# Inverted row sums are spread over their head's 64 rows through a DRAM scratch row instead of by TensorE transpositions

## The reference

```python
q  = norm(x) @ Wqa @ Wqb               # 16 heads, 128 plain + 64 rotary columns
ckv = norm(x) @ Wkva                    # 64 latent columns (keys and values) + 64 rotary ones
scores = (q_h @ k_h.T) * scale          # causal, 1024 x 1024 for each head
attn = softmax(scores)                  # exp(scores - max) / row sum
out  = attn @ v                         # v comes out of the 64 latent columns
x = x + out @ Wout
x = x + experts(norm(x))                # router, 64 experts in 8 groups, top 8
```

## Time and profile before

| | |
|---|---|
| median of 3 runs | 1745.24 us (1744.07 to 1745.45) |
| span of the profiled execution | 1743.9 us |
| attention, bodies 1 to 31 | about 36 us each, 31 times |
| PE busy | 1690.3 us, 97% |
| DVE / ACT / POOL busy | 1237.6 / 982.1 / 572.6 us |

### The profile page before, as it was taken

How to read it: one execution, slowest core, us unless ns; L and a number is a source line. 1 busy time by engine, 2 the same in 40 slices (tenths; PEclk the granted TensorE clock), 3 DMA queues, 4 the chain that set the end, 5 groups by cost and what they waited for, 6 DMA issues and landing times. The chain is left out here.

```text
span 1743.9 us, 32128 instructions
## 1 busy us (share of the span) xinstructions
PE 1690.3 (97%) x11280; PEld 1384.5 (79%) x11280; DVE 1237.6 (71%) x2858; ACT 982.1 (56%) x2319; POOL 572.6 (33%) x498
## 2 busy tenths in 40 slices
PE   5799999999999999999999999999999999999998
PEld 4677777778777777777777777777699999999998
DVE  6878788778788788787887878877654454555543
ACT  6566666666666666666666666666533333433332
POOL 4553344434443344433344334434401110110100
PEclk9899999999999999999999999999999999999999
DMA  8300000012000003000001100001200000000000
GB/s 285 123 7 7 7 14 7 8 30 76 13 8 7 7 7 103 8 7 7 9 12 49 56 7 14 7 7 42 81 1 25 25 1 25 25 13 13 13 13 13
DMA packets 35868, 51.45 MB, mean 30 GB/s; under 512 B 2368, under 2 KB 26944, under 8 KB 35712
## 3 DMA queue, kind: packets, MB, share of 16 engines
q1 hardware_dynamic: 35712, 49.39, 8.7%
HBM read 35.23 MB, written 14.16 MB: 28 GB/s over the span
## 5 line engine op out<-in xcount | busy, mean ns | idle before, releaser
L1296 ACT ACTIVATE probs<-aps,nmax 128x384 f32<-128x384 f32 (+7 forms) x512 | 378.8, 744 | 215.9 <-DVE nmax L1353 210.1
L1353 DVE CUSTOM_DVE_ANT_0 aps<-aps,mask_row 128x384 f32<-128x384 f32 (+7 forms) x512 | 388.6, 770 | 132.0 <-PE aps L43 125.7
L1222 PE MATMUL aps<-ident,probs 128*128 128x128 f32 x2304 | 329.1, 272 | 0.8 <-ACT probs L1296 0.6
L43 PE MATMUL aps<-kTh,qh 128*128 128x512 f32 (+3 forms) x768 | 293.6, 382 | 8.8 <-POOL ql L1452 3.8
L1222 PEld LDWEIGHTS aps<-ident,probs 128*128 128x128 f32 x2304 | 271.8, 140 | 23.3 <-issue 1.4
L1307 ACT COPY pT<-aps 128x512 f32<-128x512 f32 (+3 forms) x485 | 233.8, 506 | 89.1 <-PE aps L1222 86.2
L43 PE MATMUL aps<-pT,v 128*64 128x512 f32 (+3 forms) x1536 | 268.9, 492 | 0.6 <-ACT pT L1307 0.6
L43 PE MATMUL aps<-kTl,qh 128*128 128x512 f32 (+3 forms) x768 | 257.4, 343 | 0.0
L1445 POOL TENSOR_TENSOR rot<-rot 64x512 f32<-64x512 f32 x128 | 163.4, 1277 | 185.8 <-DVE rot L1367 185.8
L43 PEld LDWEIGHTS aps<-pT,v 128*64 128x64 f32 x1536 | 101.7, 136 | 152.1 <-issue 142.1
L43 PE MATMUL aps<-kTh,ql 128*128 128x512 f32 (+3 forms) x768 | 221.7, 343 | 0.0
(11 more groups left out here) (193 smaller groups left out, 3037.4 us busy)
## 6 DMA issues: line engine op xcount, KB each, us to landing
wqs<-wq_scratch SPq DMA_DIRECT2D x30, 256.0 KB, 2.6
raw_numbers<-in_x SPq DMA_DIRECT2D x8, 512.0 KB, 6.6
acc<-in_x SPq DMA_DIRECT2D x8, 512.0 KB, 3.6
x_scratch<-acc SPq DMA_DIRECT2D x8, 512.0 KB, 3.0
x<-x_scratch SPq DMA_DIRECT2D x8, 512.0 KB, 3.9
out<-x SPq DMA_DIRECT2D x7, 512.0 KB, 2.9
heads<-in_heads SPq DMA_DIRECT2D x4, 640.0 KB, 8.2
wout<-in_Wout SPq DMA_DIRECT2D x4, 512.0 KB, 8.8
```

Source lines behind the costliest of these rows:

```text
L43: return nc.tensor.matmul(out, lhsT, rhs, start=start, stop=stop, skip_group_check=True)
L1222: last = nc.tensor.transpose(tps[:, TS.index(x) % 3, j * P:(j + 1) * P], probs[c][:, c * (pair % 2), a, off:off + P], t.ident[:])
L1296: nc.scalar.activation(probs[c][:, c * (r % 2), a, off:off + w], sps[:, at:at + w], ACT.Exp, bias=nmax[:, c, a, j:j + 1], scale=-1.0, accu ...
L1353: nc.vector.tensor_tensor_reduce(out=s, in0=s, in1=mask[:, N - PW[c][j]:N], scale=-1.0, scalar=3.0e38, op0=ALU.add, op1=ALU.min, accum_out ...
```

## The change

REP, L and LOUT go, with `lrep`, `ones` and the PSUM bank slots of L. In their place SyncE does `spread_inverses(c, r)`: it waits for O(c) of the body before (the last reader of `linv_b`) and for INV(c), stores the 128x8 inverses transposed into a DRAM scratch of 8 rows of 128 numbers (each number a run of its own, four bytes), waits for the landing, and reads the 512 numbers of head 0 back into 64 partitions of `linv_b` and those of head 1 into the other 64. O(c) then waits for both reads. In SyncE's order `spread_inverses(1, r)` stands at the head of a body, ahead of `load_wq(r + 1)`, and `spread_inverses(0, r)` behind it.

```diff
-        TENSOR = [..., T(1, 3, 0), L(1), T(1, 2, 0), ..., Q(0, 0), L(0), T(1, 4, 1), ...]
+        TENSOR = [..., T(1, 3, 0), T(1, 2, 0), ..., Q(0, 0), T(1, 4, 1), ...]
-        SCALAR = [..., OUT(1, 3, 0), LOUT(1), ..., HIGH(0, 1), LOUT(0), ...]
+        SCALAR = [..., OUT(1, 3, 0), ..., HIGH(0, 1), ...]
-        POOL = [REP(1), ADD(1, 1), LOW(1, 1), ADD(1, 0), REP(0), LOW(1, 0), ...]
+        POOL = [ADD(1, 1), LOW(1, 1), ADD(1, 0), LOW(1, 0), ...]
@@ SyncE
+            def spread_inverses(c, r):
+                n = nth(c, r)
+                if n > 1:
+                    sp.wait_ge(o_sb, count(L(c), r - 1))
+                sp.wait_ge(l_inv, count(L(c), r))
+                sp.dma_start(t.l_dram[c].rearrange("m p -> p m"), linv[:, c].rearrange("p a j -> p (a j)"),
+                             allow_slow_non_contiguous=True)\
+                    .then_inc(l_kept[c], 16)
+                sp.wait_ge(l_kept[c], KEPT * n)
+                for a in range(2):
+                    row = t.l_dram[c, 4 * a:4 * a + 4].rearrange("m p -> (m p)")
+                    sp.dma_start(linv_b[64 * a:64 * a + 64, c, :], row.partition_broadcast(64)).then_inc(l_sb[c], 16)
...
+            spread_inverses(0, 0)
             for r in range(1, B * PAIRS + 1):
+                spread_inverses(1, r)
                 if r + 1 < B * PAIRS and r % PAIRS != 1 or r == 1:
                     sp.wait_ge(q_ps, max(count(Q(1, a), r - 1) for a in range(2)))
...
                     load_wq(r + 1)
...
+                if r < LAST - 1:
+                    spread_inverses(0, r)
@@ VectorE
                 def inv_job(x):
-                    if exists(L(c), r - 1):
-                        dve.wait_ge(l_rep, count(L(c), r - 1))
+                    if nth(c, r) > 1:
+                        dve.wait_ge(l_kept[c], KEPT * (nth(c, r) - 1))
                 def o_job(x):
-                    dve.wait_ge(l_sb, count(L(c), r))
+                    dve.wait_ge(l_sb[c], 32 * nth(c, r))
```

More of the change, by code:

```diff
@@ L850, in attention @@
         nmax, lsum, linv = sb("nmax", [P, 2, 2, 4]), sb("lsum", [P, 2, 2, 4]), sb("linv", [P, 2, 2, 4])
-        lrep, ones = sb("lrep", [P, 4, P]), sb("ones", [P, 1])
         linv_b = sb("linv_b", [P, 2, QC])
@@ L867, in attention @@
         s_ready, m_ready, e_done = sem("scores_ready"), sem("max_ready"), sem("exp_done")
-        l_inv, l_rep, l_ps, l_sb = (sem("rowsums_inverted"), sem("inverses_repeated"), sem("inverses_ps"),
-                                    sem("inverses_sb"))
+        l_inv = sem("rowsums_inverted")
+        l_kept = [sem("inverses_0_kept"), sem("inverses_1_kept")]
+        l_sb = [sem("inverses_0_in_sbuf"), sem("inverses_1_in_sbuf")]
         t_ready, pv_done = sem("pT_ready"), sem("pv_done")
@@ L919, in INV @@
             return ("inv", c)
-        def REP(c):
-            return ("rep", c)
-        def LOUT(c):
-            return ("lout", c)
         def O(c):
@@ L1039, in attention @@
             COUNT.update({(name, x, r): n + 1 for n, (x, r) in enumerate(done)})
+        sums = [(L(x[1]), r) for r in BODIES for x in body(VECTOR, VECTOR_FIRST, r) if x[0] == "inv"]
+        COUNT.update({("L", x, r): n + 1 for n, (x, r) in enumerate(sums)})
         def evac(x, r):
@@ L1093, in place, with nth @@
             return P if PW[c][j] == 5 * P else 0
+        KEPT = 16
+        def nth(c, r):
+            return r + age(L(c)) + 1
         @block.sync
         def _(sp):
+            def spread_inverses(c, r):
[10 more added lines that the diff above has]
+                    sp.dma_start(linv_b[64 * a:64 * a + 64, c, :], row.partition_broadcast(64)).then_inc(l_sb[c], 16)
             def load_wq(pair):
@@ L1202, in s_job @@
                     last.then_inc(s_ready, 1)
-                def l_job(x):
-                    pe.wait_ge(l_rep, count(x, r))
-                    banks_free(x)
-                    at = slot(x, r)
-                    for j in range(4):
-                        last = nc.tensor.transpose(sps[:, at + j * P:at + (j + 1) * P], lrep[:, j, :], t.ident[:])
-                    last.then_inc(l_ps, 1)
                 def t_job(x):
@@ L1269, in mask_job @@
                     mask_products(nc, t, 0, banks[:, 5, :])
-                job = {"q": q_job, "s": s_job, "l": l_job, "t": t_job, "p": pv_job, "y": y_job, "router": router_job,
+                job = {"q": q_job, "s": s_job, "t": t_job, "p": pv_job, "y": y_job, "router": router_job,
                        "mask": mask_job}
@@ L1307, in out_job @@
                     nc.scalar.copy(pT[:, k % PT_BUFS, s:QC], tps[:, k % 3, s:QC]).then_inc(t_sb["scalar"], 1)
-                def lout_job(x):
-                    _, c = x
-                    act.wait_ge(l_ps, count(L(c), r))
-                    if exists(L(c), r - 1):
-                        act.wait_ge(o_sb, count(L(c), r - 1))
-                    nc.scalar.copy(linv_b[:, c, :], sps[:, slot(L(c), r):slot(L(c), r) + QC]).then_inc(l_sb, 1)
                 def ohigh_job(x):
@@ L1321, in ohigh_job @@
                     nc.scalar.copy(oh[:, c * QC:(c + 1) * QC], o32[:, c, :]).then_inc(o_high, 1)
-                job = {"high": high_job, "exp": exp_job, "out": out_job, "lout": lout_job, "ohigh": ohigh_job}
+                job = {"high": high_job, "exp": exp_job, "out": out_job, "ohigh": ohigh_job}
                 def router_job(x):
@@ L1471, in olow_job @@
                                             ALU.subtract).then_inc(o_low, 1)
-                job = {"add": add_job, "low": low_job, "rep": rep_job, "olow": olow_job}
+                job = {"add": add_job, "low": low_job, "olow": olow_job}
+                if r == LAST:
+                    for n in FIRST_QUAD[2:]:
+                        split_first_quad(nc, t, n)
+                    router_root(nc, t, 1)
+                    for i in range(HT):
+                        router_norm(nc, t, 1, i)
                 for x in body(POOL, POOL_FIRST, r):
@@ L1486, in run @@
                             split_first_quad(nc, t, n)
-                    if r == LAST and x == REP(1):
-                        for n in FIRST_QUAD[2:]:
-                            split_first_quad(nc, t, n)
-                        router_root(nc, t, 1)
-                        for i in range(HT):
-                            router_norm(nc, t, 1, i)
             nc.gpsimd.memset(mask[:, 0:N - P], 0.0).then_inc(mask_cleared, 1)
-            nc.gpsimd.memset(ones[:], 1.0)
             nc.gpsimd.memset(t.minus_half[:], -0.5)
@@ L1832, in build @@
         t.v_dram = nc.dram_tensor("values_scratch", [2, P, NT, RANK], F32, kind="Internal").ap()
+        t.l_dram = nc.dram_tensor("inverses_scratch", [2, 8, P], F32, kind="Internal").ap()
         t.x2_dram = nc.dram_tensor("x2_scratch", [B, N, D], F32, kind="Internal").ap()
```

39 lines of the change are left out of this document (13 added, 26 removed).

## The result

| | before | changed |
|---|---|---|
| median | 1745.35 us (1744.07 to 1745.55, 4 runs) | 2011.28 us (2004.87 to 2012.10, 4 runs) |
| ratio | | 1.152 (95% interval 1.150 to 1.153) |
| span of the profiled execution | 1743.9 us | 2010.2 us |
| mean granted clock | 0.996 | 0.941 |

The change makes the kernel 266 us slower, where 30 us were forecast. The page of the changed kernel, whose first line answers to the earlier trace rows, shows three things: PE's busy time rose by 44 us although 256 matmuls are gone, its share fell from 97% to 86%, and the granted clock is down to 8 tenths in 13 of the 40 slices, where before only one read 8.

The account below looks back on a forecast made before the run. TensorE was taken to set the pace in bodies 1 to 31. Terms of -26.7 + 54 + 2 = +29 us on the 1743.9 us span gave 1773, and 1775 us as median; 8-in-10 range 1717 to 1840 us.

Parts of the forecast that it names:

- term 1: On TensorE, removing 62 L jobs in bodies 1 to 31 saves 0.43 us each: -26.7 us.
- The path to O is hidden: From INV to O, the new path takes 9.7 us against 22.4 us or more there: hidden in an ordinary body.
- The load of weights behind the detour stops TensorE: Ahead of Q(0, 1), store, reads and load take 10.5 us against 8.5 us available from INV(1)'s end.
- The store takes 4.2 us: SyncE's store of 1024 four-byte runs: 1.7 us for 128 rows plus 2.4 us for the other 896, rounded up.
- term 2: On TensorE ahead of Q(0, 1), a stop of 2.0 us in each of 27 bodies: +54 us.
- The reads take 5.3 us: SyncE's two reads of one DRAM row into 64 partitions each: 1.7 + 3.6 us, at 28 ns for each row.
- The load follows in the same queue: The query weights land 0.9 us after the reads in SyncE's queue, 6.2 us from the first read's issue.
- The clock: TensorE at half clock after a stop of more than 3 us: may come on top, no size given.
- rival B: The store is much slower, 6.5 us, so TensorE stops 4.3 us in each loading body: 1840 us, chance 0.15.
- term 3: At batch changes, bodies 9 and 17, the store stands behind keys and values: 1 us each, +2 us.

Follow-up runs that it names:

- experiment 1: The changed kernel with the load of query weights moved ahead of the spread of the c = 1 inverses in SyncE's queue: 1742.83 us, 0.9984 of before.
- experiment 3: The changed kernel with the store written as 128 runs of 32 bytes in place of 1024 of four, inverses returning in wrong order: 1731.38 us.
- experiments 4: The kernel before, with single stores of various run counts and sizes and pairs of reads timed in SyncE's idle time: 1745.88 us.
- experiment 5: The kernel before, with single stores of 1024 four-byte runs at distances of 4 to 256 bytes and pairs of reads timed: 1745.69 us.
- experiment 6: The changed kernel with the 1024 stored four-byte runs 64 bytes apart and reads from a row of another scratch: 1731.48 us.
- experiment 8: The changed kernel with 32 extra matmuls on TensorE ahead of Q(0, 1) in the 27 bodies that load there: 1975.16 us, 1.133 of before.
- experiment 9: The changed kernel with 32-byte runs stored, 4080-byte rows read back, O reading with a stride, and the weight load ahead of the spread: 1732.60 us.
- experiment 2: The changed kernel with the load of query weights issued between the store and the wait for its landing: 1905.18 us, 1.091 of before.

## Why the prediction was wrong in size, step by step

- *TensorE is the bound and L's 0.43 us count (term 1, -26.7 us).* Half right. L(1) gave its 0.43 us in each body. L(0) gave nothing: S(1, 0, 3), the job a few places behind it, had started 0.24 us after the exponentials that it waits for, the distance at which it also starts when it does wait, and comes too early for them once L(0) is gone. No wait in the profile of before names that; it is found by asking for each job behind the removed one when the thing that it waits for is ready. With 31 x 0.42 = 13 us the term was twice too large (experiments 1, 3).
- *The path to O is hidden.* Right: 9.8 us for three O jobs in the changed kernel and none for the other 61.
- *The load of weights behind the detour stops TensorE; 8.5 us are there.* Right. The first Q job starts at 698.52, and from one to the other it was 0.55 us, so Q(0, 1) would have started at 699.07, 8.5 us after INV(1) ended at 690.53; experiments 1 and 3, which take away only the lateness or only its cause, both remove the loss.
- *The store takes 4.2 us.* **This is the step that failed:** 9.4 us at the median. With 9.4 in its place the prediction's own sum gives a stop of 7.2 us (9.4 + 6.2 + 0.1 - 8.5) and 194 us for term 2, against the 202 measured. I priced a run of four bytes by the pace of loads with runs of eight bytes (2.7 ns each), as if the time were in the number of runs. The 1024 runs were through 1.6 us after the issue; the time is between them and the landing, and it depends on how close the words lie in DRAM: at the same number of runs and bytes, 10.4 us side by side and 2.6 us at 64 bytes (experiments 4 to 6). Had they been spaced, 4.2 us would have been too much.
- *The reads take 5.3 us because a row read into many partitions is slow (28 ns for each row).* Wrong in its reason: a read lands in 2.9 us alone and in 3.7 us behind the store, against 2.6 us from different rows; with the 0.5 us between the two issues that is 4.2 us for the pair in the changed kernel. What made `inv_raw` slow in the earlier trace rows isn't settled; the 1 MB issued right behind it, that I set aside, is a reading that no run tested.
- *The load follows in the same queue and lands 6.2 us after the first read's issue.* Nearly right, by luck. Over the 27 bodies the mean is 1.2 us up to the load's issue and 5.5 to its landing, 6.7 in all. With fast stores, and none close behind it, the load took 3.2 us (experiment 3), which would make 4.4. So the forecast was 1.8 us too high for the reads and the load, and left out 2.3 us by which the load is held up, most likely by the store of c = 0 behind it. By an estimate from these means (27 x 2.3), that is some 60 of the 202 us, a second cost of the same kind of store.
- *A stop of 2.0 us, 27 times (term 2, +54 us).* 202 us, or 7.5 us each, where 2.0 were forecast. Some 5.1 us of the difference are the store (9.35 us at the mean up to the first read) and some 0.5 us the rest of the chain.
- *The clock* stood in rival B as something that might come on top from a stop of 3 us, and had no term in any sum. It came, with 67 us, a quarter of the loss (experiment 8).
- *Batch changes (term 3, +2 us for bodies 9 and 17).* 2.4 us in body 9 and none in 17. Another 7.4 us came about body 24, where the spread stands behind the large loads and for which the sum had no term: 9.8 us in the changed kernel (11.4 in experiment 1).

The sum of the measured terms against the span before: 202 waits + 67 half clock - 13 for L(1) + 10 for O = 266, which is 2010.2 - 1743.9. The 67 are themselves a remainder (against experiment 1), so that the sum closes is no further proof; the 70 us of PE's busy time are the figure that stands by itself. Rival B was the one that happened, with a chance of 0.15 and a price, 1840 us, that holds for its low end.

By the fit in the Trainium skill, page "DMA: Bandwidth & Descriptors", section "Anatomy of one DMA", the store would take 2.0 us, an estimate. The trace is near it for runs of 32 bytes (1.4 us) and for spaced words (2.6 us) and 7.4 us above it for neighbouring ones (9.4 us); the measurement decides. The same section of the Trainium skill warns that the wait for the confirmation of a write can be surprisingly long, above all when the target is HBM. The trace agrees in where the time lies, behind the last packet; that it is this confirmation and nothing else, no run here shows.

## What to carry to other kernels

Before a transfer is put into a queue, list what stands behind it and when the reader of that needs it: here the detour was nearly harmless to its own reader, 22 us away, and cost 268 us through a load whose reader was 8.5 us away. Look at what stands behind it in the queue as well. Don't store single words from many partitions next to each other in DRAM when something waits for the landing: write the rows as they lie and let the reader stride (experiment 9). Spacing the words by 64 bytes made the store as harmless (experiment 6), but no run read such words back. When work is taken off the engine that sets the pace, look for the next job behind it that has to wait for another engine: here half of the gain ended there.

## What the runs showed of the hardware that I had not expected

- 128 words of four bytes, stored into one stretch of 512 bytes from 128 partitions, land in 7.4 to 8.9 us; 1024 words at 64 bytes' distance in 2.6 to 3.5; 128 runs of 32 bytes in 1.4 (experiments 4 and 5).
- The 1024 words side by side are sent within 1.6 us of the issue and land 9 us later (changed kernel, 690.6 to 701.2).
- A load of 256 KB issued 0.4 us behind such a store reaches its reader 12.7 us after its issue, against 2.6 us alone; the DMA engines' busy share is 0.28 meanwhile (experiment 2). With such a store issued 0.6 to 1.7 us behind it, a load took 3.2 to 10.7 us (changed kernel), and 3.0 to 4.0 where the stores were fast and none came close behind (experiment 3).
- A read of 2 KB out of one DRAM row into 64 partitions lands 0.3 us later than one out of 64 rows (experiment 5).
- A VectorE multiplication of 128x512 whose second operand is read with a stride of 32 bytes takes 1.12 to 1.17 us in place of 0.69 (experiment 9).
- A stop of 7.5 us on TensorE costs another 2.5 us (67 / 27) at half clock (experiment 8).
